# Mixture-of-experts routing: each indirect scatter waits for the one before it

## The chip, the cores and the metric

The kernel runs on one core of a Trainium2 chip. The metric is the device time of one execution in microseconds (us), the median of several runs. Lower is better. A profile is a separate execution, recorded by the hardware profiler.

## The reference

Eight sublayers run over x of shape (32, 128, 256): four layers, each a cross-attention sublayer and a feed-forward sublayer. Layers 1 and 3 have a mixture of experts as feed-forward, 8 experts with the 2 best of them for each token. Layer 1's, cut to what matters:

```
logits = einsum('bsd,de->bse', x, Wg) + bg
topk_vals, topk_idx = top_k(logits, 2);  topk_w = softmax(topk_vals)
h  = relu(einsum('bsd,edf->bsef', x, W1) + b1)
eo = einsum('bsef,efd->bsed', h, W2) + b2
mixed = sum(take_along_axis(eo, topk_idx) * topk_w)
return gamma * norm(mixed + x) + beta          # x here is layernorm(x)
```

Layer 3's is the same in form: router, top two, a gated unit (silu(gate) * up) in each expert, weighted sum.

## The kernel before

The 4096 tokens stand as 32 columns of 128 rows in on-chip memory; a row is 256 float32, 1 KB. The phases run one after another: `L0x`, `L0f`, `L1x`, `L1f`, `L2x`, `L2f`, `L3x`, `L3f` (x is attention, f feed-forward). Each phase is made of blocks. At the end of a block all engines meet in a barrier, so nothing of the next block starts before the slowest engine is through.

The mixture phases are `experts_phase`, for `L1f` and for `L3f`. It has three parts:

- `prepare`: normalizes the tokens into `kept`, computes router logits (TensorE), the top two and, for every token and choice, the row number `slot` at which the token goes into a list sorted by expert (VectorE). When `slot` is written, VectorE raises the semaphore `placed`. Then GpSimd copies the rows: one indirect DMA for each column and choice, 128 rows of 1 KB each, 128 KB in all, from `kept` to the DRAM list `rows_in`. All of them raise one semaphore, `scattered`, by 16 each.
- `compute_tiles` (L1f, 72 tiles) or `compute_half_tiles` (L3f, 2 times 40 tiles): the expert products on tiles of 128 sorted rows. SyncE loads the tiles from `rows_in`.
- the weighted sum: in L1f it is done in the following phase, in L3f by `combine`.

`HALF` is the number of columns that `prepare` scatters: 32 in L1f, so 64 scatters; 16 in L3f, so 32 scatters. The other 16 columns of L3f are scattered by GpSimd in `compute_half_tiles` (line 2171), beside the first tiles; these lines are the same before and after the change.

In L1f, `prepare` has other work to hide behind. `keys_ahead` is true there: TensorE projects the keys of the following attention in 128 steps (line 1848), ScalarE copies each result out of PSUM (line 1803), and SyncE stores every four of them, 512 KB, to DRAM (line 1769). In L3f there is no such work, and `keys_ahead` is false.

The instructions that end a block bear the line of its opening `with` (1709 for `prepare`): a branch, a DRAIN, and the semaphores of the barrier. Lines 136 and 137 clear the semaphores of the block and meet once more.

Of the kernel before, what the change touches and what calls it, by code (L numbers as in the profile page):

```python
# [1698 lines left out]
def prepare(nc, sh, phase, w, c, lg, gate, slot, share, expert, kept, rows_in, next_phase):  # L1699
# [5 lines left out]
    HALF = BATCH // halves  # L1705
# [3 lines left out]
    with ExitStack() as ctx:  # L1709
# [17 lines left out]
        placed, scattered = core.sem("slots_ready"), core.sem("rows_scattered")  # L1727
# [23 lines left out]
        if keys_ahead:  # L1751
            @block.sync
            def _(sp):
                def load(g):
                    sp.dma_start(cT[:, g % 2, :, :], sh.dram["ctxT"][:, :, g * T:(g + 1) * T]).then_inc(ctx_loaded[g % 2], 16)

                load(0)
                sh.load_columns(sp, next_phase, KEY_COLUMNS, 2 * KEY_COLUMNS, wk_loaded)
                load(1)
                sh.loads[next_phase] = 32  # L1760
                for at in (0, 2 * KEY_COLUMNS):
                    sh.load_columns(sp, next_phase, at, KEY_COLUMNS if at == 0 else columns(next_phase), sh.loaded[next_phase])
                for n in range(HALVES):
                    g, half = n // 2, n % 2
                    if half and g + 2 < HALVES // 2:
                        sp.wait_ge(projected, KTILES * (n + 1))
                        load(g + 2)
                    sp.wait_ge(keys_out, KTILES * (n + 1))
                    sp.dma_start(sh.dram["keysT"][:, half, KG * g:KG * (g + 1), :],
                                 keys[:, n % 2, :, :, :].rearrange("p j t q -> p j (t q)")).then_inc(keys_stored[n % 2], 16)  # L1770
                for k in range(2):
                    sp.wait_ge(keys_stored[k], HALVES // 2 * 16)
# [5 lines left out]
        @block.gpsimd  # L1778
        def _(pool):

            pool.wait_ge(placed, 1)
            for b in range(HALF):
                for k in range(2):
                    pool.indirect_dma_start(out=rows_in[0], out_offset=bass.IndirectOffsetOnAxis(ap=slot[:, k, b:b + 1], axis=0),
                                            in_=kept[:, b, :], in_offset=None).then_inc(scattered, 16)
            pool.wait_ge(scattered, 2 * HALF * 16)

        @block.scalar
# [1464 lines left out]
```

## Time and profile before

| | us |
|---|---|
| median of 3 runs | 3513.22 |
| lowest and highest run | 3511.18, 3513.64 |
| span of the profiled execution | 3632.7 |

The profiled execution has no time but its span. It is 119.5 us longer than the median of the timed runs. In the profile TensorE is busy for 3010.8 us (83%), VectorE for 2320.2 (64%), ScalarE for 1697.5 (47%), GpSimd for 1319.8 (36%). The share of busy time is a mean over very different stages; what a change in one block is worth is read from that block: which engine arrives last at its barrier.

### The profile page before, as it was taken

The page shows a single profiled execution, that of the slowest core. Times are in us where ns is not written, and L with a number is a line of the kernel's source. Part 1 is how long each engine was busy: PE and PEld are TensorE (multiplying, and loading weights), DVE is VectorE, ACT ScalarE, POOL GpSimd, SP SyncE. Part 2 cuts the span into 40 slices and gives each one's busy share as a digit, 9 for nine tenths or more (in the row PEclk, how much of TensorE's full clock was granted, in tenths as well). Part 3 has the DMA queues.
Part 4 walks back from the last instruction along what each step waited for, and adds up shares of the span by engine and source line. Part 5 has one row for each costly group of instructions (what it writes and reads, how often), then busy time and mean ns, then how long its engine had stood idle before and what let it go on. Part 6 is the DMA issues. An engine that isn't in the chain of part 4 may idle for free. (4 is left out here: it accounts for less than half of the span.)

```text
span 3632.7 us, 74176 instructions
## 1 busy us (share of the span) xinstructions
PE 3010.8 (83%) x24093; PEld 2134.9 (59%) x24102; DVE 2320.2 (64%) x5140; ACT 1697.5 (47%) x2908; POOL 1319.8 (36%) x1326
## 2 busy tenths in 40 slices
PE   6996899999979998399978999995564899835983
PEld 5885232232238887289966777773343677624883
DVE  6887566666335664014438888877997899832564
ACT  4774788888834442033323444442444566510110
POOL 1111455556514440520003333320435677533023
PEclk9998999999989997599989999997787899967997
DMA  2001444444333203332231111110000433112334
GB/s 102 16 14 34 118 133 121 124 125 130 99 142 117 100 18 126 126 138 72 70 123 51 56 51 53 50 40 16 1 0 19 175 117 117 65 41 94 98 103 133
DMA packets 196205, 302.07 MB, mean 83 GB/s; under 512 B 24560, under 2 KB 133232, under 8 KB 189808
## 3 DMA queue, kind: packets, MB, share of 16 engines
q1 hardware_dynamic: 183648, 266.40, 23.4%
q0 software_dynamic: 12432, 34.10, 2.9%
q8 instruction: 67, 1.10, 0.1%
q14 instruction: 58, 0.48, 0.0%
HBM read 216.51 MB, written 75.50 MB: 80 GB/s over the span
## 5 line engine op out<-in xcount | busy, mean ns | idle before, releaser
L2518 ACT ACTIVATE params<-L0f_Z,params 128x1024 f32<-128x1024 f32 x512 | 532.6, 1113 | 83.9 <-PE L0f_Z L2574 83.7
L2495 POOL TENSOR_TENSOR L0f_mixed<-L0f_mixed,L0f_gated 128x512 f32<-128x512 f32 x240 | 332.1, 1384 | 291.6 <-DVE L0f_gated L2738 291.3
L2574 PE MATMUL L0f_Z<-params,L0f_w_stacked 128*128 128x512 f16 x1024 | 296.9, 388 | 34.1 <-ACT params L2518 23.2
L2738 DVE SCALAR_TENSOR_TENSOR L0f_gated<-L0f_O,params 128x512 f32<-128x512 f32 x240 | 180.0, 750 | 224.0 <-PE L0f_O L2583 147.9
L2583 PE MATMUL L0f_O<-params 128*32 128x512 f32 x2048 | 275.1, 609 | 0.4 <-ACT params L2518 0.4
L860 POOL TENSOR_TENSOR params<-params,L2x_recip_den 128x512 f32<-128x512 f32 x128 | 134.8, 1053 | 353.8 <-DVE L2x_recip_den L1115 353.3
L2574 PEld LDWEIGHTS L0f_Z<-params,L0f_w_stacked 128*128 128x128 f16 x1024 | 70.6, 98 | 289.6 <-ACT params L2518 265.9
L2209 PE MATMUL L3ftiles_H<-L3ftiles_rowsT,L3ftiles_w_tile 128*128 128x128 f32 x1296 | 166.9, 284 | 51.0 <-DVE L3ftiles_rowsT L2237 36.0
L2209 PEld LDWEIGHTS L3ftiles_H<-L3ftiles_rowsT,L3ftiles_w_tile 128*128 128x128 f32 x1296 | 161.8, 199 | 63.1 <-DVE L3ftiles_rowsT L2237 41.1
L2880 POOL TENSOR_SCALAR L2f_hidden_int<-params 128x1024 bf16<-128x1024 f32 x32 | 119.2, 3724 | 200.1 <-ACT params L2907 198.2
L1848 PE MATMUL L1fprepare_K<-L1fprepare_ctxT,params 128*128 128x256 f32 x512 | 130.1, 414 | 59.4 <-issue 51.4
L2016 ACT ACTIVATE L1ftiles_hidden<-L1ftiles_H,L1ftiles_b_tile 128x128 f32<-128x128 f32 x292 | 83.2, 367 | 198.6 <-PE L1ftiles_H L2036 198.6
L854 POOL DMA_INDIRECT L2x_gathered<-rows_out_dram,L1f_slots x64 | 64.2, 1003 | 289.6 <-POOLq L137 258.3
L2189 ACT ACTIVATE L3ftiles_silu<-L3ftiles_H 128x256 f32<-128x256 f32 x81 | 31.0, 383 | 265.8 <-PE L3ftiles_H L2209 202.3
L1848 PEld LDWEIGHTS L1fprepare_K<-L1fprepare_ctxT,params 128*128 128x128 f32 x512 | 103.3, 207 | 80.3 <-issue 66.3
L2036 PEld LDWEIGHTS L1ftiles_H<-L1ftiles_rowsT,L1ftiles_w_tile 128*128 128x128 f32 x1168 | 145.0, 196 | 5.4 <-DVE L1ftiles_rowsT L2064 1.8
L2036 PE MATMUL L1ftiles_H<-L1ftiles_rowsT,L1ftiles_w_tile 128*128 128x128 f32 x1168 | 145.9, 280 | 1.0 <-DVE L1ftiles_rowsT L2064 1.0
L2077 DVE COPY L1ftiles_b_tile<-params 128x4 f32 x74 | 15.0, 203 | 203.3 <-issue 202.6
L1569 DVE TENSOR_TENSOR L1x_products<-L1x_S,const_sb 128x512 f32<-128x512 f32 x128 | 82.5, 686 | 91.9 <-PE L1x_S L1479 91.9
L893 ACT ACTIVATE params<-params 128x512 f32<-128x512 f32 x128 | 79.9, 624 | 130.2 <-DVE params L1107 130.2
L956 PE MATMUL L2x_gen<-L2x_xnT,params 128*128 128x128 f32 x1024 | 130.5, 282 | 7.0 <-DVE L2x_xnT L1098 7.0
L2046 PE MATMUL L1ftiles_Y<-params,L1ftiles_hidden 128*128 x576 | 136.3, 380 | 0.0
(508 smaller groups left out, 7698.5 us busy)
## 6 DMA issues: line engine op xcount, KB each, us to landing
params<-gates_dram SPq DMA_DIRECT2D x512, 128.0 KB, 3.2
params<-side_dram SPq DMA_DIRECT2D x32, 1024.0 KB, 4.8
keysT_dram<-L1fprepare_keysT SPq DMA_DIRECT2D x32, 512.0 KB
params<-keysT_dram SPq DMA_DIRECT2D x32, 512.0 KB
rows_in_dram<-L1x_zero SPq DMA_DIRECT2D x30, 512.0 KB, 3.3
L3ftiles_rows<-rows_in_dram SPq DMA_DIRECT2D x84, 128.0 KB
rows_out_dram<-L3ftiles_outputs SPq DMA_DIRECT2D x80, 128.0 KB
L1ftiles_rows<-rows_in_dram SPq DMA_DIRECT2D x76, 128.0 KB
```

The lines of the kernel that those rows point to most:

```text
L860: pool.tensor_tensor(p[:, g, :, :], p[:, g, :, :], rc[:, g, :].unsqueeze(2).broadcast_to([P, UH, P]), ALU.mult).then_inc(divided, 1)
L956: mm = pe.matmul(banks.at(chunk)[:, t * P:(t + 1) * P], w["wq"][:, k, (n * BT + t) * P:(n * BT + t + 1) * P], xnT[:, k, :], start=(k == 0) ...
L1848: mm = pe.matmul(K[:, t, :], wk[:, k, tile * P:(tile + 1) * P], cT[:, g % 2, k, :], start=(k == 0), stop=(k == KT - 1))
L2036: mm = pe.matmul(H[:, b.slot, f, :], w1[:, b.slot, k, f * P:(f + 1) * P], rT[:, b.slot, k, :], start=(k == 0), stop=(k == KT - 1))
L2046: mm = pe.matmul(Y[:, b.slot, 0:D], hid[:, b.slot, f, :], w["w2"][:, bass.ds(e, 1), f, :].rearrange("p a d -> p (a d)"), start=(f == 0), s ...
L2209: mm = pe.matmul(H[:, b.slot, f, :], w1[:, b.slot, k, f * P:(f + 1) * P], rT[:, b.slot, k, :], start=(k == 0), stop=(k == KT - 1))
L2495: pool.tensor_tensor(acc[:, b.slot, m % KT, :], acc[:, b.slot, m % KT, :], tmp[:, m % 2, :], ALU.add).then_inc(mixed, 1)
L2518: act.activation(hid[:, n % 4, :, :], Z[:, n % 2, :, :], ACT.Gelu, bias=w["b1"][:, n // 4:n // 4 + 1]).then_inc(hid_ready, 1)
L2574: mm = pe.matmul(Z[:, n % 2, s, :], w1s[:, e, :], stack[:, b.slot, t, 2 * half + s, :], start=True, stop=True)
L2583: mm = pe.matmul(O[at:at + 32, m % 2, :], w["w2"][:, e, :], hid[:, (2 * m + q // 2) % 4, q % 2, :], start=True, stop=True)
L2738: dve.scalar_tensor_tensor(out=out, in0=O[:, m % 2, :], scalar=w["b2"][:, e:e + 1], in1=gb[:, e % AHEAD, m % KT, :], op0=ALU.add, op1=ALU. ...
L2880: pool.tensor_scalar(hq[:, j, :], h[:, b.slot, j, :], -ROUND, 127.0, ALU.add, ALU.min).then_inc(hq_ready, 1)
```

## The change

In `prepare`, the two loops over columns and choices become one loop over n. Before each scatter but the first, GpSimd waits until `scattered` has reached 16 times the number of scatters issued, that is until all earlier ones have landed. Which rows go where, the number of DMAs and their order stay the same. `prepare` serves both mixture phases, so the waits are in L1f (63 of them) and in L3f (31).

```
-            for b in range(HALF):
-                for k in range(2):
-                    pool.indirect_dma_start(out=rows_in[0], out_offset=bass.IndirectOffsetOnAxis(ap=slot[:, k, b:b + 1], axis=0),
-                                            in_=kept[:, b, :], in_offset=None).then_inc(scattered, 16)
+            for n in range(2 * HALF):
+                b, k = n // 2, n % 2
+                if n:
+                    pool.wait_ge(scattered, n * 16)
+                pool.indirect_dma_start(out=rows_in[0], out_offset=bass.IndirectOffsetOnAxis(ap=slot[:, k, b:b + 1], axis=0),
+                                        in_=kept[:, b, :], in_offset=None).then_inc(scattered, 16)
             pool.wait_ge(scattered, 2 * HALF * 16)
```

## Rows read from the trace of the kernel before

**Rows 1.** The changed line: duration ns min/median/max, first and last start.

```profile
L1784 POOL DMA_INDIRECT rows_in_dram<-L1f_normalized,L1f_slots x64: 956/960/1653, 1442.9 to 1523.3; - x64
L1784 POOL DMA_INDIRECT rows_in_dram<-L3f_normalized,L3f_slots x32: 956/960/1299, 3232.8 to 3272.5; - x32
```

**Rows 2.** Timeline of GpSimd in L1f: start, duration, idle before.

```profile
1442.94 1.65 POOL L1784 DMA_INDIRECT rows_in_dram<-L1f_normalized,L1f_slots  x1 [86.72 <-DVEq L1945]
1444.89 0.97 POOL L1784 DMA_INDIRECT rows_in_dram<-L1f_normalized,L1f_slots  x1 [0.30 <-issue]
...
1523.28 0.96 POOL L1784 DMA_INDIRECT rows_in_dram<-L1f_normalized,L1f_slots  x1 [0.30 <-issue]
```

**Rows 3.** Timeline where L1f's prepare ends and its tiles begin.

```profile
1600.01 0.38 ACT L1803 ACTIVATE L1fprepare_keysT<-L1fprepare_K 128x256 f32<-128x256 f32 x1 [0.48 <-PE L1fprepare_K L1848]
1600.41 0.33 SPq L1769 DMA_DIRECT2D keysT_dram<-L1fprepare_keysT  x1
1604.21 1.91 SPq L1987 DMA_DIRECT2D L1ftiles_rows<-rows_in_dram  x4
```

**Rows 4.** Timeline where L3f's prepare begins to scatter and where it ends.

```profile
3232.27 0.18 DVE L1944 TENSOR_SCALAR L3f_slots<-L3fprepare_second 128x32 int32<-128x32 f32 x1
3232.80 1.30 POOL L1784 DMA_INDIRECT rows_in_dram<-L3f_normalized,L3f_slots  x1 [79.25 <-DVEq L1945]
...
3271.21 0.96 POOL L1784 DMA_INDIRECT rows_in_dram<-L3f_normalized,L3f_slots  x1 [0.30 <-issue]
3272.47 0.96 POOL L1784 DMA_INDIRECT rows_in_dram<-L3f_normalized,L3f_slots  x1 [0.30 <-issue]
3278.46 0.82 SPq L2140 DMA_DIRECT2D L3ftiles_rows<-rows_in_dram  x2
```

**Rows 5.** GpSimd's queue at the end of both prepares: ns, first and last start.

```profile
L1709 POOLq COMPARE_BRANCH  x2: 38/40/43, 1525.7 to 3274.9; - x2
L1709 POOLq DRAIN  x2: 2665/3974/5282, 1525.9 to 3275.1; - x2
```

**Rows 6.** DMA engines from 3254.77 to 3258.77, in 40 slices of 0.1 us.

```profile
DMA  0069981000000009696000000000996300000000
```

**Rows 7.** Timeline of the last gather in combine, and who waited for it.

```profile
3621.63 0.95 POOL L2336 DMA_INDIRECT L3fcombine_gathered<-rows_out_dram,L3f_slots  x1 [0.30 <-issue]
3624.58 1.67 DVE L2355 SCALAR_TENSOR_TENSOR L3fcombine_mixed<-L3fcombine_gathered,L3fcombine_shares_now,x_sb 128x256 f32<-128x256 f32 x4 [6.58 <-DMA L3fcombine_gathered<-rows_out_dram,L3f_slots]
```

**Rows 8.** Busy time by stretch: PE, PEld, DVE, ACT, POOL, clock, DMA share, GB/s.

```profile
1443.00:1455.00 12.00, 12.00 (x57) 10.60 (x56) 1.51 (x3) 4.21 (x12) 9.28 (x9) 1.00 0.73 262
1455.00:1534.00 79.00, 19.94 (x43) 11.28 (x41) 0.00 (x0) 4.06 (x11) 52.76 (x55) 0.52 0.32 116
1545.00:1600.00 55.00, 54.97 (x255) 48.15 (x253) 0.00 (x0) 24.02 (x64) 0.00 (x0) 1.00 0.51 186
3232.80:3278.50 45.70, 0.00 (x0) 0.00 (x0) 2.51 (x6) 0.04 (x1) 31.18 (x32) 0.50 0.26 92
3288.50:3324.50 36.00, 5.74 (x26) 4.86 (x24) 1.87 (x4) 0.39 (x2) 24.23 (x25) 0.59 0.29 102
3334.50:3344.50 10.00, 10.00 (x77) 9.57 (x76) 6.94 (x15) 1.53 (x4) 0.00 (x0) 1.00 0.30 96
```

**Rows 9.** Timeline of ScalarE in L1f's prepare, while GpSimd scatters and after.

```profile
1477.56 0.38 ACT L1803 ACTIVATE L1fprepare_keysT<-L1fprepare_K 128x256 f32<-128x256 f32 x1 [8.72 <-issue]
1488.08 0.38 ACT L1803 ACTIVATE L1fprepare_keysT<-L1fprepare_K 128x256 f32<-128x256 f32 x1 [10.14 <-DMA gates_dram<-L0f_gatesT]
...
1545.62 0.38 ACT L1803 ACTIVATE L1fprepare_keysT<-L1fprepare_K 128x256 f32<-128x256 f32 x1 [0.48 <-PE L1fprepare_K L1848]
1546.48 0.38 ACT L1803 ACTIVATE L1fprepare_keysT<-L1fprepare_K 128x256 f32<-128x256 f32 x1 [0.48 <-PE L1fprepare_K L1848]
```

**Rows 10.** DMA engines from 1545.34 to 1553.34, in 40 slices of 0.2 us.

```profile
DMA  0003784799999988100069999980010000000059
```

## The prediction

> **What bounds the kernel now.** I looked for the changed line first. It runs 64 times in L1f and 32 times in L3f [rows 1], so one edit has to be read in two places. The timeline shows the pace: GpSimd is busy 0.96 us with a scatter, pauses 0.30 us, and issues the next, waiting for nothing [rows 2, 4]. From 3232.80 to 3272.47 that is 39.67 us for 31 intervals, 1.28 us each.
>
> Then I asked, at each place, who comes last to the barrier. In L3f it is GpSimd: between 3232.80 and 3278.50 TensorE and ScalarE do nothing, VectorE has 2.5 us of work, GpSimd 31 us [rows 8]. Every microsecond added there is added to the kernel. In L1f GpSimd issues its last scatter at 1523.28 [rows 2], but the key projection goes on until 1600.01 and the tiles begin at 1604.21 [rows 3]. By this profile there are some 70 us of cover.
>
> That cover is doubtful. From 1455 to 1534 the projection nearly stands: 11 steps of ScalarE in 79 us, against 64 in 55 us (0.86 us each) once the scatters are over [rows 8]; one step starts 10.5 us after the other, where 0.86 is usual [rows 9]. So 79 - 11 x 0.86 = 69.5 us are lost. The same is seen in L3f from 3288.5 to 3324.5, beside the scatters of line 2171: 26 matmuls in 36 us, where 77 go into 10 us later [rows 8], which loses 36 - 26 x 0.13 = 32.6 us. DMA engines are only 0.3 busy in both stretches, so they aren't full. Together 102 us, and the profiled execution is 119.5 us longer than the timed ones. The likeliest reading is that most of this standstill belongs to the recorded execution alone, and that in a timed run L1f's tiles begin near 1604.2 - 69.5 = 1534.7 on this scale. GpSimd would be through at 1523.28 + 8.6 = 1531.9 (8.6 is worked out below): there is next to no cover.
>
> **The change, part by part.** The loop over n in place of two loops costs nothing: the code is unrolled, and the DMAs and their order are the same. Added are 63 waits in L1f and 31 in L3f. Behind the waiting instruction stands only the rest of GpSimd's own scatters and the block's end; all other engines wait for that at the barrier.
>
> *The interval T between two scatters.* GpSimd already waits once for a landing, at the end of each prepare. The last scatter starts at 1523.28 and at 3272.47; GpSimd's next instruction, the branch, starts at 1525.7 and 3274.9 [rows 2, 4, 5]: 2.42 and 2.43 us. The DMA engines agree: in steady state each scatter's packets take some 0.6 us, one burst every 1.27 us [rows 6], so nothing is queued and a lone scatter lands as fast as one in the stream. After the wait the next scatter has to be dispatched; the nearest rows are the 0.30 us pause between two scatters [rows 2] and 3232.80 - 3232.45 = 0.35 us from VectorE's last write to the first scatter [rows 4], part of which is the semaphore's way, already in 2.42. The lower bound of T is 2.42, and I take 2.6. For the upper bound: the first scatter after a long idle takes 1.65 and 1.30 us instead of 0.96 [rows 2, 4], 0.5 more on average. If every wait brought that back, T = 3.1. A gather as seen by VectorE takes 3624.58 - 3621.63 = 2.95 us [rows 7], inside these bounds.
>
> The Trainium skill, "DMA: Bandwidth & Descriptors", section on the anatomy of one DMA on the GpSimd path, fits one such DMA as 2.0 us plus bytes over 436 GB/s, which is an estimate of 2.3 us for 131,072 bytes, most of it the write's receipt. Counted from the issue it agrees with the 2.42 us of the row. Counted from the end of the 0.96 us for which GpSimd is busy, it would make T about 3.4 and the sum below 207 us in place of 131; the branch at +2.42 speaks against that.
>
> *The tail.* From the last scatter's start to the next block's first load L3f takes 3278.46 - 3272.47 = 5.99 us [rows 4]. In it lies a DRAIN. There are two, of 2665 and 5282 ns [rows 5]; the one at 3275.1 must be the short one, for 3275.1 + 5.28 is past 3278.46. So the DRAIN takes 5.28 us after 64 scatters and 2.67 after 32, 0.083 us a scatter. In L3f it is on the path before and after. In L1f it is hidden now (it ends at 1531.2), and comes into the open if GpSimd becomes last: the tail there is 5.99 - 2.67 + 5.28 = 8.6 us. I assume that it counts DMAs and so doesn't shrink; if it does, it takes at most 5.3 and 2.7 us off.
>
> *Contention.* While the projection runs at full speed the DMA engines are 0.51 busy without any scatter [rows 8]; a store is a burst of some 1.5 us [rows 10]. A scatter that meets one waits about half of it: 1.5/3.45 (four steps of 0.86 us are one store) x 0.75 = 0.33 us on average. Before, that was hidden in the stream. Until 1534.7 some 31 scatters are issued: 10 us, between 0 and 25.
>
> *Sum for L3f*, whatever the standstill is: 31 x 2.6 - 39.67 = +40.9 us.
>
> *Sum for L1f*: the last scatter starts at 1442.94 + 63 x 2.6 + 10 = 1616.7, the tiles at 1625.3. Against 1534.7 that is +90.6 us. The clock at the tiles' start doesn't differ by more than a microsecond or two, since the stage begins after an idle TensorE either way.
>
> Together +131.5 us on the timed 3513.2: **3645 us**, 3.7% slower. The span of a profile should grow less, by 21 + 41 = 62 us to about 3695: there the 70 us are cover.
>
> **The rivals.**
>
> *The standstill is real in timed runs too.* Then L1f's tiles begin at 1604.2 before and 1625.3 after, +21.1, and with L3f +62: 3575 us. For it: nothing in the rows says that the recording causes it. Against it: the 119.5 us, which would want another source. The Trainium skill, "NOTIFIC — Programmer's Manual", section 1.1, says that an engine that reports an event has already moved on when the record is written and never blocks on the host. By that rule recording would cost little, and this rival would win; no run here shows it yet.
>
> *Every wait restarts GpSimd cold* (T = 3.1). L1f: 1442.94 + 195.3 + 10 + 8.6 = 1656.8, +122.1; L3f: 96.1 - 39.7 = +56.4; together +178.5, 3692 us. For it: the slow first scatters. Against it: those come after 80 us of idleness, not after 1.5.
>
> *Paced scatters free the projection, and the kernel gets faster.* The standstill is real and vanishes when only one scatter is in flight; the projection ends by 1534.7. L1f then gains if 1442.94 + 63T + 8.6 is under 1604.2, and the whole gains if 94T is under 192.4, that is T below 2.05. At T = 1.9: L1f -33, L3f +19.2, 3499 us. Against it: the 2.42 us seen twice.
>
> *The waits are passed at once* because the landing is earlier than the next issue: T stays 1.28, no change. The same 2.42 us excludes it nearly.
>
> **How the numbers follow.** The forecast has 0.60, with a range of its own from T = 2.42 without contention (L1f 1604.0 - 1534.7 = +69.3, L3f +35.3: 3618) to 3692. The real standstill has 0.23, the cold restart 0.12, the faster case 0.02, no change 0.02; 0.01 is left for others. The range 3560 to 3705 takes in the first three with their bounds, but for the real standstill with T near 2.42 (+36, 3549). A measurement of this kernel can tell about 0.2%, 7 us: slower 0.96, same 0.02, faster 0.02.
>
> **What would show it.** In the changed profile: intervals between scatters of 2.5 to 2.8 us in L3f, somewhat longer in L1f up to about 1535; a DRAIN of 5.3 us that now ends just before the tiles' first load; the projection at 0.86 us a step throughout, if it is the dense stream that halts it. The span against the timed median tells the two main cases apart: if the standstill belongs to recording, the difference shrinks from 119 us to about 50, what line 2171 leaves. The prediction is wrong if T is far from 2.6, or if the timed time rises by only some 60 us.

## The result, and the profile after

The changed kernel takes 3666.1 us (3662.6 to 3670.0, 4 runs) against 3512.3 us for the kernel before on the same chip: 1.0441 times as long, 95% interval 1.0428 to 1.0453. That is +153.9 us. The forecast was 3645 us, +131.5, in a range of 3560 to 3705. In one later run a single execution of ten took 6561.0 us, the other nine 3505 to 3511 us; its ratio leaves that one out.

The changed line is now 1786. Its row, as in [rows 1], and the first and some later scatters of L1f, as in [rows 2]; the last column says how long GpSimd idled and what ended it:

```profile
L1786 POOL DMA_INDIRECT rows_in_dram<-L1f_normalized,L1f_slots x64: 958/959/1657, 1442.1 to 1637.4; - x64
L1786 POOL DMA_INDIRECT rows_in_dram<-L3f_normalized,L3f_slots x32: 958/959/1301, 3271.3 to 3354.3; - x32
```

```profile
1442.12 1.66 POOL L1786 DMA_INDIRECT rows_in_dram<-L1f_normalized,L1f_slots  x1 [86.66 <-DVEq L1947]
1446.37 0.97 POOL L1786 DMA_INDIRECT rows_in_dram<-L1f_normalized,L1f_slots  x1 [2.59 <-DMA rows_in_dram<-L1f_normalized,L1f_slots]
...
1502.41 0.96 POOL L1786 DMA_INDIRECT rows_in_dram<-L1f_normalized,L1f_slots  x1 [1.70 <-DMA rows_in_dram<-L1f_normalized,L1f_slots]
1508.57 0.96 POOL L1786 DMA_INDIRECT rows_in_dram<-L1f_normalized,L1f_slots  x1 [5.20 <-DMA rows_in_dram<-L1f_normalized,L1f_slots]
1512.40 0.96 POOL L1786 DMA_INDIRECT rows_in_dram<-L1f_normalized,L1f_slots  x1 [2.88 <-DMA rows_in_dram<-L1f_normalized,L1f_slots]
...
1637.44 0.96 POOL L1786 DMA_INDIRECT rows_in_dram<-L1f_normalized,L1f_slots  x1 [1.70 <-DMA rows_in_dram<-L1f_normalized,L1f_slots]
```

The pause was 0.30 us, put down to "issue"; now it is 1.70 us or more, and a landing ends it. In L3f the pause is 1.70 to 1.72 us throughout:

```profile
3274.34 0.98 POOL L1786 DMA_INDIRECT rows_in_dram<-L3f_normalized,L3f_slots  x1 [1.71 <-DMA rows_in_dram<-L3f_normalized,L3f_slots]
3277.04 0.96 POOL L1786 DMA_INDIRECT rows_in_dram<-L3f_normalized,L3f_slots  x1 [1.71 <-DMA rows_in_dram<-L3f_normalized,L3f_slots]
...
3354.35 0.96 POOL L1786 DMA_INDIRECT rows_in_dram<-L3f_normalized,L3f_slots  x1 [1.71 <-DMA rows_in_dram<-L3f_normalized,L3f_slots]
```

The end of L1f's prepare, as in [rows 3], is the last step of the projection and the first load of the tiles; then GpSimd's queue, as in [rows 5]:

```profile
1529.61 0.39 ACT L1805 ACTIVATE L1fprepare_keysT<-L1fprepare_K 128x256 f32<-128x256 f32 x1 [0.48 <-PE L1fprepare_K L1850]
...
1646.06 3.40 SPq L1989 DMA_DIRECT2D L1ftiles_rows<-rows_in_dram  x5
```

```profile
L1709 POOLq COMPARE_BRANCH  x2: 38/40/43, 1639.9 to 3356.8; - x2
L1709 POOLq DRAIN  x2: 2665/3974/5282, 1640.0 to 3356.9; - x2
```

The projection is through at 1530; everything then waits 116 us for GpSimd. By stretch, as in [rows 8]:

```profile
1442.00:1533.00 91.00, 87.32 (x403) 75.94 (x401) 1.70 (x3) 37.93 (x102) 23.74 (x24) 1.00 0.59 220
1533.00:1640.00 107.00, 0.00 (x0) 0.00 (x0) 0.00 (x0) 0.00 (x0) 38.36 (x40) 0.50 0.14 49
```

The columns are the length of the stretch, then busy time of TensorE, its weight loads, VectorE, ScalarE and GpSimd, the granted clock, the DMA share and GB/s. In the second stretch only GpSimd works, 0.96 us out of every 2.67, and the DMA engines are 0.14 busy: this is pure waiting.

The span of this profile is 3665.5 us, the same as the timed runs. It is itself the profile of one of the four timed executions, the one of 3667.4 us; the first profile of the kernel before has no time of its own, and was 119.5 us longer than the timed runs. So the rise of the span (+33) and the rise of the time (+154) differ, and the difference had to be settled first.

### The profile page after: what moved, and what is told of

Same layout as the page of the kernel before. It is cut to its first block and busy times, and to the rows that moved or that the text cites. A ratio compares the mean times of both kernels' runs of the same rounds, so it can differ in the third digit from the quotient of the medians.

```text
span 3665.5 us, 74176 instructions
## 1 busy us (share of the span) xinstructions
PE 2993.0 (82%) x24093; PEld 2125.6 (58%) x24102; DVE 2320.7 (63%) x5140; ACT 1697.1 (46%) x2908; POOL 1323.6 (36%) x1326
## 3 DMA queue, kind: packets, MB, share of 16 engines
q1 hardware_dynamic: 183648, 266.40, 22.7%
## 5 line engine op out<-in xcount | busy, mean ns | idle before, releaser
L1786 POOL DMA_INDIRECT rows_in_dram<-L1f_normalized,L1f_slots x64 | 62.1, 970 | 220.8 <-DMA rows_in_dram<-L1f_normalized,L1f_slots 134.2
L1569 DVE TENSOR_TENSOR L1x_products<-L1x_S,const_sb 128x512 f32<-128x512 f32 x128 | 82.4, 686 | 91.8 <-PE L1x_S L1479 91.8
L2252 DVE COPY L3ftiles_w_tile<-params 128x1024 f32 x82 | 57.3, 699 | 129.9 <-PEq L137 87.3
```

## The experiments

Two lengths are read in every run: from the first scatter to the first load of the next block's tiles, in L1f and in L3f. In the changed kernel they are 1646.06 - 1442.12 = 203.9 us and 3360.33 - 3271.34 = 89.0 us. The time is a median. Each ratio is to the kernel before on the same chip (medians 3510.9 to 3512.9 us); the last two rows have only two executions each.

| run | L1f, us | L3f, us | time, us | ratio to before (95%) |
|---|---|---|---|---|
| before, first profile | 161.3 | 45.7 | 3512.3 | |
| before again | 90.8 | 45.7 | 3511.3 | 0.9997 (0.9987 to 1.0007) |
| changed | 203.9 | 89.0 | 3666.1 | 1.0441 (1.0428 to 1.0453) |
| waits in L1f only | 199.3 | 45.8 | 3617.8 | 1.0303 (1.0286 to 1.0320) |
| waits in L3f only | 89.1 | 89.0 | 3556.2 | 1.0129 (1.0112 to 1.0146) |
| two in flight | 122.3 | 47.8 | 3545.6 | 1.0100 (1.0083 to 1.0117) |
| four in flight | 91.7 | 45.8 | 3514.4 | 1.0005 (0.9996 to 1.0015) |
| waits, key stores cut | 187.5 | 89.0 | 3652.4 | 1.0401 (1.0384 to 1.0418) |
| no waits, key stores cut | 89.0 | 45.6 | 3508.2 | 0.9988 (0.9978 to 0.9998) |
| waits, 64 of 128 rows | 191.8 | 84.6 | 3653.9 | 1.0399 (1.0381 to 1.0416) |
| waits, stores and loads cut | 180.1 | 88.9 | 3645.1 | 1.0385 (1.0355 to 1.0415) |
| waits, loads cut | 197.6 | 88.9 | 3661.2 | 1.0431 (1.0400 to 1.0461) |

**The kernel before, again.** No edit.

> The kernel before, unchanged, profiled once more. Theory 'one odd execution': the standstill of 102 us in the first profile (69.5 us in L1f beside the dense scatters, 32.6 us and more in L3f beside those of line 2171) belongs to that execution and not to the kernel. Then this profile has a span near 3510 us, the key projection runs at 0.86 us a step throughout, and L1f's tiles begin about 91 us after its first scatter. Theory 'recording': the standstill comes whenever dense scatters are recorded. Then the span is again near 3630 us and the tiles begin some 161 us after the first scatter. The timed median is about 3512 us by both.

Its span is 3511.3 us. The changed line, and stretches that answer to the two standstills of [rows 8] (the second one starts with its block, 10 us earlier than the row of before):

```profile
L1784 POOL DMA_INDIRECT rows_in_dram<-L1f_normalized,L1f_slots x64: 959/963/1657, 1444.7 to 1525.3; - x64
```

```profile
1444.00:1530.00 86.00, 84.96 (x392) 73.93 (x391) 2.13 (x5) 35.98 (x98) 62.30 (x64) 1.00 0.77 282
3209.00:3245.00 36.00, 33.29 (x240) 31.40 (x241) 20.88 (x44) 5.15 (x12) 27.75 (x27) 0.91 0.54 176
```

The scatters are as dense as ever (64 in 80.6 us), and beside them ScalarE makes 98 steps in 86 us at full clock, where the first profile had 11 in 79 us. L1f's tiles start 90.8 us after the first scatter; I had worked out 1534.7 - 1442.94 = 91.8 by taking the standstill away. So there was next to no cover in the timed runs (GpSimd's own scatters and tail take 80.6 + 8.6 = 89.2 us), and the standstill is neither a property of the kernel nor of being profiled: it belonged to that one execution. None of the other profiles of this study shows it, though line 2171's scatters are dense in all of them: from L3f's first tile load to the end of the span they take 302 to 305 us, the first profile 3632.7 - 3278.46 = 354.2. So the standstill was 161.3 - 90.8 = 70.5 us in L1f and 49 to 52 in L3f, where I had counted 32.6 to 3324.5 only; together they account for the 119.5 us. The rest of L3f's part shows when the steps of ScalarE and the tile loads of the two profiles are laid side by side. In L3f the first profile loses 35 us by 3335, nearly all of it beside the scatters, then nothing up to 3431, then 16 us between 3432 and 3563, where GpSimd issues the gathers of line 2181. The second of these two steps of ScalarE comes 9.48 us after the first, where 2.87 is usual there; eight gathers are issued from 3439.5 to 3448.5:

```profile
3441.58 0.38 ACT L2189 ACTIVATE L3ftiles_silu<-L3ftiles_H 128x256 f32<-128x256 f32 x1 [2.99 <-PE L3ftiles_H L2209]
3451.06 0.38 ACT L2189 ACTIVATE L3ftiles_silu<-L3ftiles_H 128x256 f32<-128x256 f32 x1 [9.10 <-DMA L3x_ctxT<-ctxT_dram]
```

So in that execution the other engines lost their time while GpSimd issued indirect DMAs, scatters and gathers alike. Why in that execution alone stays open.

**Waits in one phase only.**

```
-                if n:
+                if n and keys_ahead:          # L1f only
-                if n:
+                if n and not keys_ahead:      # L3f only
                     pool.wait_ge(scattered, n * 16)
```

> Waits in L1f only, L3f dense as before. My account of the changed kernel: L1f's part is 204 us from first scatter to first tile load (63 x 2.667 + 27 of contention + 8.6 of tail) against about 92 before, so +112, and the timed time is 3512 + 112 = 3624 us. Rival 'the cover of 70 us was real': +43 and 3555 us, and most of the 154 us would have to come from L3f.

> Waits in L3f only, L1f dense. My account: 31 x (2.667 - 1.28) = +43 us, 3555 us. Rival 'the cover was real': the remainder of the 154 us, +111 and 3623 us. The two parts should add up: the excesses of this run and of the one with waits in L1f only sum to 154 us if they don't touch each other.

L1f alone costs 3617.8 - 3512.9 = +105 us, L3f alone 3556.2 - 3512.9 = +43 us. The expected 3624 and 3555 were met within 6 and 1 us. The sum, 148 us, is 6 us short of 154; the L1f stretch itself differs by 4.6 us between two executions with the same code in it (203.9 and 199.3), so I take no meaning from that. The rival with real cover, 3555 and 3623, is ruled out.

**Two and four in flight.** One semaphore for each residue of n, so that each wait is for one known scatter (only the waits are shown; each scatter raises the semaphore of its own residue):

```
-                if n:
-                    pool.wait_ge(scattered, n * 16)
+                if n > 1:                                   # four: n > 3, n % 4, n // 4
+                    pool.wait_ge(scattered[n % 2], n // 2 * 16)
```

> Each scatter waits for the one before last, with a semaphore of its own for even and odd scatters, in both phases; two are in flight. Theory 'the cost is the landing's latency': the interval is the larger of 1.27 (issue) and 2.667 / 2 = 1.33 us, so L3f costs 31 x 0.06 = 2 us more than before, L1f 63 x 0.06 = 4 us and a part of the contention, up to 20 us; 3515 to 3535 us. Rival 'every wait costs, whatever it waits for' (a restart of GpSimd): the interval stays above 2 us even with two in flight, and the time above 3580 us.

> Each scatter waits for the fourth before it, one semaphore for each residue of four. In L3f the interval is 1.27 to 1.28 us, no cost. In L1f two in flight left 30 us of delay from meeting stores; four cover 4 x 1.27 = 5.1 us, as long as the slowest landings of the changed kernel (a gap of 5.2 us), so nearly all of it goes: tiles at 91 to 95 us after the first scatter, time 3512 to 3518 us. If the delay were a matter of the DMA engines' load and not of waiting, it would stay near 30 us and the time near 3543 us.

With two in flight, the row of the changed line and three of its pauses in L3f:

```profile
L1786 POOL DMA_INDIRECT rows_in_dram<-L3f_normalized,L3f_slots x32: 954/958/1299, 3194.0 to 3235.8; - x32
```

```profile
3209.11 0.96 POOL L1786 DMA_INDIRECT rows_in_dram<-L3f_normalized,L3f_slots  x1 [0.43 <-DMA rows_in_dram<-L3f_normalized,L3f_slots]
3210.38 0.96 POOL L1786 DMA_INDIRECT rows_in_dram<-L3f_normalized,L3f_slots  x1 [0.31 <-DMA rows_in_dram<-L3f_normalized,L3f_slots]
3211.76 0.96 POOL L1786 DMA_INDIRECT rows_in_dram<-L3f_normalized,L3f_slots  x1 [0.43 <-DMA rows_in_dram<-L3f_normalized,L3f_slots]
```

The interval is 41.8 / 31 = 1.35 us, against 1.33 expected: a wait costs nothing in itself, only the landing does. L3f costs 2.1 us, as expected. L1f costs 31 us where at most 24 had been expected, and the time of 3545.6 us is outside the expected 3515 to 3535: while stores pass, one pause is 4.08 us long, and a second scatter in flight doesn't bridge it.

```profile
1481.74 0.96 POOL L1786 DMA_INDIRECT rows_in_dram<-L1f_normalized,L1f_slots  x1 [0.30 <-issue]
1486.78 0.96 POOL L1786 DMA_INDIRECT rows_in_dram<-L1f_normalized,L1f_slots  x1 [4.08 <-DMA rows_in_dram<-L1f_normalized,L1f_slots]
```

Four in flight nearly bridge it. GpSimd's idle time before the scatters, grouped by what ended it:

```profile
  issue: 27.1, 89
  DMA rows_in_dram<-L1f_normalized,L1f_slots: 4.2, 5
```

Only 5 of 94 pauses still end with a landing, 4.2 us in all, and the time is that of the kernel before, within an interval that reaches 0.15%, 5 us. So "not before the fourth one back has landed" costs nothing that can be measured here, and "not before the last one has landed" costs 154 us. They are not the same order: the first leaves up to four scatters under way at once.

**Key stores cut down, with and without waits.** 64 KB are stored where it was 512 KB; zeros are stored in the list during L1x (not shown; endings of lines left out):

```
-   sp.dma_start(sh.dram["keysT"][:, half, KG * g:KG * (g + 1), :],
-                keys[:, n % 2, :, :, :].rearrange("p j t q -> p j (t q)"))
+   sp.dma_start(sh.dram["keysT"][:, half, KG * g, 0:P], keys[:, n % 2, 0, 0, :])
```

> The changed kernel with the 32 stores of projected keys (512 KB each) in L1f's prepare cut down to 64 KB each; zeros are stored in the key list during L1x instead, so that the following attention works on keys that are mostly zero. The 16 loads of 256 KB stay. Theory 'a scatter that waits for its landing also waits for the store it meets': of the 27 us that L1f's interval adds to 63 x 2.667, at least 20 go; from the first scatter to the tiles' first load it takes 177 to 184 us, where the changed kernel takes 204. Rival 'the scatters are slower in L1f for another reason' (TensorE and ScalarE at work, the loads): it stays above 195 us. The timed time isn't compared with the changed kernel's but with that of the dense twin of this run.

> The kernel before with the same stores cut down and the same zeros stored in L1x: the dense twin. By my account dense scatters hide the stores, so that from the first scatter to the tiles nothing changes: 91 us, set by the key projection. The waits then cost (177 to 184) - 91 + 43 = 129 to 136 us between this run and its twin with waits, where they cost 154 us with the stores in place.

The 63 intervals of 2.667 us and the tail of 8.6 us make 176.6 us for L1f; the changed kernel is 27.3 us above that. Without the stores the stretch is 187.5 us: 16.4 of the 27.3 us went, less than the 20 I had set as the least. In the dense twin it is 89.0 us, 2 under the expected 91: GpSimd's own 80.4 us of scatters and 8.6 of tail are as long as that, so GpSimd and the projection come in together. The waits cost 3652.4 - 3508.2 = 144 us there, above the expected 129 to 136. The stores are the larger part of the delay, and something else is left. That led to the next pair.

**Context loads cut down as well, or alone.** The 14 loads after the first two carry 32 KB instead of 256 KB (endings of lines left out).

```
                 def load(g):
-                    sp.dma_start(cT[:, g % 2, :, :], sh.dram["ctxT"][:, :, g * T:(g + 1) * T])
+                    t = T if g < 2 else T // 8
+                    sp.dma_start(cT[:, g % 2, :, 0:t], sh.dram["ctxT"][:, :, g * T:g * T + t])
```

> The changed kernel with L1f's key stores cut to 64 KB as before, and 14 of the 16 context loads beside them cut from 256 KB to 32 KB (the key projection then works in part on old context). With the stores cut alone, 187.5 us were left from the first scatter to the tiles, 10.9 above 63 x 2.667 + 8.6 = 176.6. Theory 'the remainder is the loads': it falls to 177 to 180 us. Rival 'the remainder is the projection itself' (TensorE and ScalarE reading and writing on-chip memory, or the semaphores): it stays near 187 us.

> The changed kernel with the 14 context loads cut to 32 KB and the full 512 KB stores. If loads and stores delay the scatters independently, the first scatter to the tiles takes 204 - 11 = 193 us. If a scatter is delayed only once by a load and the store issued half a microsecond after it, the loads hide behind the stores and it stays at 198 to 204 us.

With both cut it is 180.1 us, at the edge of the expected 177 to 180: of the 27.3 us, 16.4 went with the stores, 7.4 with the loads, and 3.5 are left, with 64 KB stores and 32 KB loads still passing. While the projection runs, 17 pauses are more than 0.2 us over 1.70 in the changed kernel, 12 without the stores and 2 without both. The projection ran at its full pace in these kernels (0.86 us a step), so it isn't its work that delays the scatters. With the loads alone cut it is 197.6 us, between the two cases that I had set apart (193, and 198 to 204). Given that equal code differed by 4.6 us, that run is inconclusive on whether loads and stores delay independently, and how the 23.8 us divide between the two is known no better.

There is a third kind of DMA that no run took away. The profile has a queue 8, named instruction, that moves a packet of 16 KB now and then. In the changed kernel three pauses hold such a packet, and they are the three longest, 4.59, 5.09 and 5.20 us; the other 21 pauses up to the projection's end are 3.95 us at most, 2.51 on average. The last of the three, 1504.5 to 1505.5:

```profile
q1 hardware_dynamic: 86, 0.29, 72.9%
q0 software_dynamic: 26, 0.09, 23.0%
q8 instruction: 1, 0.02, 5.8%
```

With two in flight the three longest pauses (3.64, 4.01 and 4.08 us) are again those with such a packet, and the other pauses are 2.46 at most. Without stores and loads one pause stays long, 3.74 us, and a packet of queue 8 starts in it, at 1503.56; but two more pauses there have such a packet and are 1.74 and 1.99 us. So some 3 x (4.96 - 1.70) = 10 of the 27.3 us fall into pauses in which such a packet passes beside the stores and loads. In six of the seven profiles with one or two scatters in flight in L1f the longest pause has one in it. That is a coincidence in time; whether the packet is a cause wasn't tested.

**Half the rows.** Slots and rows are taken from partitions 0 to 63 only (cut to the two arguments that change):

```
-   ap=slot[:, k, b:b + 1] ... in_=kept[:, b, :]
+   ap=slot[0:P // 2, k, b:b + 1] ... in_=kept[0:P // 2, b, :]
```

> The changed kernel with only the first 64 of each column's 128 rows scattered, 64 KB instead of 128 KB; the other rows of the list stay zero. Theory 'the interval is latency': the interval in L3f falls only by the shorter burst and a shorter issue, from 2.67 to 2.1 to 2.5 us, L3f's part by 5 to 17 us. Rival 'the interval is work by bytes': it halves to 1.33 us, and the whole change costs nothing in L3f any more.

```profile
3271.13 0.89 POOL L1786 DMA_INDIRECT rows_in_dram<-L3f_normalized,L3f_slots  x1 [1.64 <-DMA rows_in_dram<-L3f_normalized,L3f_slots]
3273.67 0.89 POOL L1786 DMA_INDIRECT rows_in_dram<-L3f_normalized,L3f_slots  x1 [1.64 <-DMA rows_in_dram<-L3f_normalized,L3f_slots]
```

```profile
L1709 POOLq DRAIN  x2: 2665/3974/5282, 1630.9 to 3346.9; - x2
```

Half the bytes take 0.14 us off the interval of 2.67 (0.07 off the busy time, 0.07 off the pause), to 2.53, a little less than I had expected. The interval is latency, not bytes. The DRAIN is unchanged to the nanosecond, so it doesn't go by rows or bytes.

Other blocks of the same traces show that it goes by the number of indirect DMAs. These are three more DRAINs of GpSimd, from the repeated profile of the kernel before:

```profile
L789 POOLq DRAIN  x1: 6414/6414/6414, 2400.5 to 2400.5; - x1
L2108 POOLq DRAIN  x1: 10399/10399/10399, 3428.7 to 3428.7; - x1
L2828 POOLq DRAIN  x1: 11369/11369/11369, 2721.5 to 2721.5; - x1
```

Each begins while work issued earlier still runs on GpSimd, so what counts is how long it goes on after the last of that work. It is 5.31 us in line 789's block, which has 64 gathers, 5.29 us in line 2108's, which has 32 scatters and 32 gathers, and 0.07 us in line 2828's, which has none. That holds to 0.01 us in all twelve profiles.

## Why the prediction was right, and where it was off

**What bounds, and where.** Right, and it carried the most: the edit was read in both phases, and the 70 us of apparent cover in L1f were refused. With the cover believed, the forecast would have been 3575 us, which is one of the rivals; the repeated profile and the two one-phase kernels rule it out. The reason given for refusing it was half wrong, and that it cost nothing was luck: any cause that keeps the standstill out of the timed runs gives the same forecast. "Most of this standstill belongs to the recorded execution alone" holds for that one execution, but I had thought that recording brings it on, and that the changed kernel's profile would still be 50 us longer than its runs. It is not longer at all (3665.5 and 3666.1), nor is that of the kernel before when taken again (3511.3 and 3511.3). The rule cited from the Trainium skill, "NOTIFIC — Programmer's Manual", section 1.1, that an engine which reports an event never blocks on the host, agrees with these four numbers, but they don't test it: both profiles are of executions that are themselves among the timed ones. It didn't follow that the standstill was in the timed runs: I had weighed two explanations, and it was a third, a single disturbed execution.

**The interval T.** Forecast 2.6 us in 2.42 to 3.1; measured 83.0 / 31 = 2.68, first interval with its cold start included, and 2.67 in the stream. It is 0.96 us of issue and 1.71 of pause. The cold-restart rival (T = 3.1, 3692 us) is ruled out: after a pause of 1.7 us a scatter still takes 0.96 us. The time alone wouldn't have done it, since 3666 us lies about midway between that rival and the forecast. This term was 2.4 us short in L3f (+43.3 measured, 89.0 - 45.7, against +40.9) and 63 x 0.07 = 4 us short in L1f.

**The tail.** Forecast 8.6 us in L1f and 5.99 in L3f; measured 1646.06 - 1637.44 = 8.62 and 3360.33 - 3354.35 = 5.98. The DRAIN of 5.28 us came into the open as said. That it goes by the number of DMAs was an assumption from two rows; the half-row run and the blocks of lines 789, 2108 and 2828 support it.

**Contention.** This is the mis-sized term: forecast 10 us (0 to 25), measured 204 - 63 x 2.667 - 8.6 = 27.3, and 22.7 in the run with waits in L1f only. The step that failed is that a scatter which meets a store "waits about half of" a burst, 0.33 us on average. About 24 scatters shared 27.3 us, 1.1 us each, and one pause grew by 3.5 us. By the runs that cut them, stores and loads together account for 23.8 of it; in the three longest pauses they met a packet of the instruction queue, whose part wasn't tested. How a scatter's packets are interleaved with the others wasn't shown.

**The sum.** L1f: +113.1 measured (203.9 - 90.8) against +90.6: contention 17, T 4, and 1 from the start of the tiles before (90.8 for 91.8). L3f: +43.3 against +40.9. Together 156.4 from two profiles, 153.9 from the timed runs, 131.5 forecast.

**The faster rival** needed T under 2.05, and real cover. Neither was there.

## What to carry to other kernels

A wait for the landing of every DMA makes the whole latency the interval: 2.67 us instead of 1.28, and with half the bytes still 2.53. Ask how far back the order has to reach. Two in flight took the interval to 1.35 us in a quiet stretch, and four hid even most of the landings that other DMAs delayed. Before work is counted as cover, ask whether the timed runs have it: a span that is longer than the timed runs is a sign that some stretch of the profile isn't in them, and a second profile shows which. When one function serves two phases, price the edit in each: here L3f, which has no other work to hide behind, paid 43 of the 154 us.

## What the runs showed of the hardware

- The DRAIN that closes a block on GpSimd takes 2665 ns after 32 indirect DMAs and 5282 ns after 64, within 5 ns in all twelve profiles, with 128 or 64 rows a DMA, and after all of them had landed: 0.082 to 0.083 us for each DMA issued. In two other blocks with 64 indirect DMAs the DRAIN goes on for 5.29 and 5.31 us after GpSimd's last work, in blocks without any for 0.07 to 0.17 us. A third block, with 32 gathers, has 3.03 to 3.19 us.
- A lone indirect scatter of 128 rows has an interval of 2.67 us, of 64 rows 2.53. Beside 512 KB stores and 256 KB loads issued by SyncE, the pause before the next grew from 1.70 to 2.51 us on average and 3.95 at most, and to 4.59, 5.09 and 5.20 us where a 16 KB packet of the instruction queue was moved too.
- In one profiled execution of the kernel before, the engines with work beside GpSimd's scatters and gathers lost some 120 us (70 in L1f, some 50 in L3f), in L1f at a DMA share of 0.32. None of the eleven later profiles repeated it. Its cause stays open.
